# A two-bank rotation for every product of a Gelu stage, its folds by transfers and GpSimd additions, and both halves of the output product in one run

## The chip, the cores and the metric

The kernel runs on one NeuronCore of a Trainium2 chip. The metric is the device time of one execution in microseconds (us). The engines are named as the profile names them: PE (TensorE, matrix products), PEld (its weight loads), ACT (ScalarE), DVE (VectorE), POOL (GpSimd), and SP (SyncE, which issues nearly all transfers here). Each engine works through its own list of instructions in order; the lists meet only at semaphores.

## The reference, cut to what matters

The program is two blocks of a network over `x` of 32 images, 256 channels, 14 by 14 points. The change lies in the last part, a mixture of experts over 8 heads of 32 channels, 16 experts each, on 6272 tokens:

```
h = x @ Wm + bm
t = h.reshape(bs * L_ * H, HD)                      # H = 8 heads of HD = 32
w = softmax(t @ expert_emb); topw, topi = top_k(w, 2)
hmid = gelu(einsum('td,edi->tei', t, W1) + b1)      # 16 experts, 128 hidden each
eo = einsum('tei,eio->teo', hmid, W2) + b2          # back to 32 per head
comb = (sel * topw[:, :, None]).sum(axis=1)         # sel: eo at the two best experts
out = comb.reshape(bs, L_, d) @ Wo + bo             # then added to the residual
```

The kernel computes all 16 experts and multiplies each by a gate that is zero except at the two best, so the sum over `sel` is a sum over the 16 experts.

## The kernel before, in words

The Gelu stage is the last part of the program and takes its last 900 us or so. Its work is cut into 49 **units** of 1024 columns (256 tokens by 4 heads; the last unit has 128 tokens by 8 heads). Each unit has 4 **groups** of 4 experts, so there are 196 groups. The order of the work is a loop over **slots** k on every engine: slot k holds the first products of group k and the second products of group k-1.

- `first(m)` (L2265, PE): for expert m the product with W1, 2 matmuls of 512 columns, into one of three double banks of PSUM, `psA`. ACT's Gelu (L2326) reads that double bank and writes `hid`. `first` waits until the Gelu three experts back is done.
- `second(g, b)` (L2275, PE): for half b (512 columns) of group g the products of its four experts with W2, side by side in the array, into one of two single banks, `psY`. `weigh` (L2347, DVE) adds b2, multiplies by the gates and frees the bank. A plain slot on PE is first, first, first, second half 0, first, second half 1.
- The first group of a unit is weighed into `gacc`, the other three into two buffers `gsum`, and POOL adds each of these to `gacc` (L2254). `weigh` of a unit's last group waits for POOL's addition of the group two before it (`Q["acc"]` at `a - 1`): it writes into that buffer.
- `fold` (L2286, PE): four matmuls with a matrix of ones and zeros add up the four groups of 32 partitions of `gacc` (four experts apart) and put the heads in their places, into a `psY` bank; `combine` (L2356, DVE) copies the 256 columns to `comb`. It runs in slot 4w+6.
- `last` (L2296, PE) and `finish` (L2363, DVE): the product with Wo for 256 tokens, half m_ of the output channels in each of two slots (8c+11 and 8c+12), then bias and residual; SP stores it (L2241). `fold` and `last` take their turn in the `psY` banks as well.
- The routing of later tokens runs alongside: 16 small DVE steps per chunk (`route`, L1625 to L1648), four transposes (L1661), a copy, and a store of the gates.
- SP's list per slot: at every fourth slot `heads_load` (L2205, 4 transfers), then `gates_load` for group k+2 (L2215, 4 transfers, into one of three buffers; it waits until group k-1 is weighed), then the stores of that slot. Waits are put into the list by a helper at L48.

Of the kernel before, what the change touches and what calls it, by code (L numbers as in the profile page):

```python
# [81 lines left out]
def build(nc, x, c1T, c2T, c3T, invts, lut1, lut2, lut3, bn1, bn2, bn3, routerT, w_moe,  # L82
          se_w1T, se_b1, se_w2T, se_b2, se_wgT, se_bg, wm, bm, emb, w1, b1, w2, b2, wo, bo, out):
    with ExitStack() as ctx:
# [990 lines left out]
        Q = {k: sem(f"q_{k}") for k in ("w", "w2", "wo", "set", "hi", "mm1", "gel", "put", "got", "acc", "rt")}  # L1075
# [4 lines left out]
        q_st = [sem(f"q_st{a}") for a in range(2)]  # L1080
        w1_r = sb("w1_r", [128, NE, HID], F32R)
# [3 lines left out]
        foldm = sb("fold", [128, HD])  # L1085
# [523 lines left out]
        def gates_ps(use):  # L1609

            return ps4[:, 3, 64:64 + CH] if use < EARLY else psY[use % 2]
# [44 lines left out]
        def route_pe(eng, r, use):  # L1656

            wait(eng, Q["rt"], (r + 1) * RT2)
            wait(eng, Q["got"], use if r < EARLY else use - 1)
# [63 lines left out]
        with nc.Block() as block:  # L1723
# [34 lines left out]
            def _(eng):  # L1758
# [4 lines left out]
                eng.memset(foldm[:], 0.0).then_inc(Q["set"], 1)  # L1763
                for r in range(4):
                    eng.wait_ge(Q["set"], r + 3)

                    eng.affine_select(out=foldm[:], in_=foldm[:], compare_op=ALU.not_equal, fill=1.0,
                                      base=-32 * r, pattern=[[-1, HD]], channel_multiplier=1).then_inc(Q["set"], 1)
# [368 lines left out]
        comb = ex[:].rearrange("p h c -> p (h c)")[:, 0:2 * UT].rearrange("p (a c) -> p a c", a=2)  # L2137
# [4 lines left out]
        psA = [ctx.enter_context(nc.psum_tensor(f"psA{a}", [128, NB * BLK], F32)) for a in range(3)]  # L2142
        psY = [ctx.enter_context(nc.psum_tensor(f"psY{a}", [128, BLK], F32)) for a in range(2)]
# [5 lines left out]
        FOLD = {4 * w + 6: w for w in range(NU)}  # L2149
        LAST = {8 * c + 11 + m_: (c, m_) for c in range(len(PARTS) - 1) for m_ in range(2)}  # L2150
        LAST.update({4 * NU + 3 + m_: (len(PARTS) - 1, m_) for m_ in range(2)})
# [4 lines left out]
        for r in reversed(range(EARLY, T)):  # L2156
            over = min(over, NEEDED[r] - 6)
            while over + 2 in FOLD or over + 2 in LAST:
                over -= 1
# [3 lines left out]
            clear = [k for k in range(over, over + PACE) if k + 1 not in LAST]  # L2163
# [5 lines left out]
        EXTRAS, EXTRA_USE, BLOCK_USE, uses = {}, {}, {}, EARLY  # L2169
        for k in range(SLOTS):  # L2170
            EXTRAS[k] = [kind for kind, table in (("last", LAST), ("route", ROUTE), ("fold", FOLD)) if k in table]
            for kind in EXTRAS[k]:
                EXTRA_USE[kind, k] = uses
                uses += 1
            for b in range(NB if 0 < k <= NG else 0):
                BLOCK_USE[k - 1, b] = uses
                uses += 1

        def apart(k):

            return not EXTRAS[k] or (EXTRAS[k] == ["fold"] and k + 1 not in LAST)

# [13 lines left out]
        def tokens(c):  # L2196
            tok, n = PARTS[c]
            return V[:].rearrange("p h t c -> p h (t c)")[:, :, tok:tok + n]

# [18 lines left out]
        with nc.Block() as block:  # L2218
            @block.sync
            def _(eng):  # L2220
# [5 lines left out]
                for k in range(SLOTS):  # L2226
# [6 lines left out]
                    if k + 2 < NG:  # L2233

                        wait(eng, q_wst, stored_gates(sum(need <= k + 2 for need in NEEDED)))
                        gates_load(eng, k + 2)
                    if k in LAST:
                        c, m_ = LAST[k]
                        wait(eng, Q["got"], EXTRA_USE["last", k] + 1)
                        for image, at_, off, n in STORES[c]:  # L2240
                            eng.dma_start(out[image, m_ * 128:(m_ + 1) * 128, at_:at_ + n],  # L2241
                                          fin[:, m_, off:off + n]).then_inc(q_st[m_], 16)
# [4 lines left out]
            def _(eng):  # L2247
                for w in range(NU):
                    for g in range(1, 4):
                        a = 3 * w + g - 1  # L2250

# [176 lines left out]
```

## Time and profile before

| what | value |
|---|---|
| median of 3 runs | 2328.03 us (2325.78 to 2329.89) |
| the profiled execution, its own time | 2325.96 us |
| its span in the profile | 2324.2 us |
| busy share of the span: PE, DVE, ACT, POOL | 88%, 58%, 55%, 36% |
| Gelu instructions (ACT L2326) | 784, 809.7 us busy |

The profiled execution is 2.07 us below the median of the three runs, and its span leaves 1.76 us of its time uncovered. Busy shares are averages over stages with different limits. In the last 900 us ACT and PE are the busy ones. SP's issuing instructions are not counted as busy; how full SP is has to be read from its timeline and its waits.

### The profile page before, as it was taken

The page shows a single profiled execution, that of the slowest core. Times are in us where ns is not written, and L with a number is a line of the kernel's source. Part 1 is how long each engine was busy: PE and PEld are TensorE (multiplying, and loading weights), DVE is VectorE, ACT ScalarE, POOL GpSimd, SP SyncE. Part 2 cuts the span into 40 slices and gives each one's busy share as a digit, 9 for nine tenths or more (in the row PEclk, how much of TensorE's full clock was granted, in tenths as well). Part 3 has the DMA queues.
Part 4 walks back from the last instruction along what each step waited for, and adds up shares of the span by engine and source line. Part 5 has one row for each costly group of instructions (what it writes and reads, how often), then busy time and mean ns, then how long its engine had stood idle before and what let it go on. Part 6 is the DMA issues. An engine that isn't in the chain of part 4 may idle for free. (4 is left out here: it accounts for less than half of the span.)

```text
span 2324.2 us, 36023 instructions
## 1 busy us (share of the span) xinstructions
PE 2050.6 (88%) x12850; PEld 1136.7 (49%) x12851; DVE 1336.8 (58%) x2117; ACT 1286.3 (55%) x1634; POOL 831.9 (36%) x608
## 2 busy tenths in 40 slices
PE   6999699999796783798499986999999999999998
PEld 3444355555454562677266553444444444444444
DVE  5666435554456874222388963666666666667533
ACT  3444312222354331122245425999989989999897
POOL 4333111211000777000688611444334443343443
PEclk8999869999798765999689988999999999999999
DMA  2110121220613442677324325666565666556654
GB/s 57 29 29 15 48 85 58 67 69 20 245 55 113 142 146 77 170 210 207 102 83 136 118 73 154 157 158 165 157 164 157 156 162 165 162 152 158 158 155 106
DMA packets 280563, 281.24 MB, mean 121 GB/s; under 512 B 44998, under 2 KB 261654, under 8 KB 280278
## 3 DMA queue, kind: packets, MB, share of 16 engines
q1 hardware_dynamic: 246422, 233.49, 36.6%
q0 software_dynamic: 12288, 25.72, 3.7%
q10 hardware_dynamic: 21696, 19.93, 2.5%
q8 instruction: 99, 1.62, 0.3%
q14 instruction: 58, 0.48, 0.1%
HBM read 203.76 MB, written 75.25 MB: 120 GB/s over the span
## 5 line engine op out<-in xcount | busy, mean ns | idle before, releaser
L2326 ACT ACTIVATE BIG<-psA,b_s 128x1024 f32<-128x1024 f32 x784 | 809.7, 1116 | 88.7 <-PE psA L2265 81.1
L2254 POOL TENSOR_TENSOR BIG<-BIG 128x1024 f32<-128x1024 f32 x147 | 359.4, 2445 | 552.1 <-DVE BIG L2347 552.1
L2265 PE MATMUL psA<-x_r,w_r 128*128 128x512 f32 x1568 | 479.7, 427 | 20.3 <-DMA x_r<-hs_d 12.1
L2347 DVE SCALAR_TENSOR_TENSOR BIG<-psY,b_s,BIG 128x512 f32<-128x512 f32 x392 | 291.6, 750 | 246.2 <-PE psY L2275 245.4
L2265 PEld LDWEIGHTS psA<-x_r,w_r 128*128 128x128 f32 x1568 | 268.7, 190 | 329.4 <-ACT BIG L2326 248.2
L2275 PE MATMUL psY<-BIG,w_s 128*32 128x512 f32 x3136 | 399.9, 600 | 3.6 <-DVE BIG L2347 2.9
L719 DVE TENSOR_REDUCE b_nm<-psN 112x32 f32<-112x512 f32 x128 | 83.1, 686 | 148.0 <-PE psN L616 147.6
L1199 POOL DMA_INDIRECT xg_d<-xnb,SLOT x128 | 135.1, 1056 | 80.8 <-DVE SLOT L1314 44.2
L1774 POOL DMA_INDIRECT gath<-yg_d,SLOT x128 | 140.1, 1095 | 38.5 <-issue 35.7
L2275 PEld LDWEIGHTS psY<-BIG,w_s 128*32 128x32 f32 x3136 | 73.5, 108 | 161.2 <-issue 90.5
L719 DVE TENSOR_REDUCE a_nm<-psN 98x32 f32<-98x512 f32 x128 | 82.4, 686 | 87.5 <-PE psN L607 87.3
L557 POOL CAST b_pat_r<-BIG 72x3584 fp32r<-72x3584 f32 x16 | 50.7, 3171 | 219.5 <-PE psN L616 212.6
L1535 PE MATMUL ps<-BIG,xv 128*128 x528 | 126.6, 383 | 2.2 <-ACT xv L1561 1.0
L1561 ACT ACTIVATE xv<-ps 128x512 f32<-128x512 f32 x66 | 39.4, 597 | 157.5 <-PE ps L1521 155.7
L775 ACT ACTIVATE b_exs<-ps 128x1568 f32<-128x1568 f32 x32 | 47.3, 1477 | 104.6 <-PE ps L585 104.6
L580 PE MATMUL ps<-BIG,b_wb 72*128 72x392 f32 x256 | 101.0, 541 | 4.0 <-DVE xv L725 4.0
L1535 PEld LDWEIGHTS ps<-BIG,xv 128*128 128x128 f32 x528 | 96.1, 192 | 14.2 <-issue 3.7
L1576 DVE COPY ex<-ps 128x512 f32<-128x512 f32 x33 | 22.8, 692 | 99.7 <-PE ps L1535 99.7
L616 PE MATMUL psN<-b_wb_r,b_pat_r 73*112 73x128 f32 x512 | 70.6, 285 | 9.3 <-POOL b_pat_r L557 8.5
L1521 PE MATMUL ps<-ident,xv 128*128 128x128 f32 x264 | 41.3, 281 | 41.1 <-DMA xv<-xg_d 25.3
L616 PEld LDWEIGHTS psN<-b_wb_r,b_pat_r 73*112 73x112 f32 x512 | 61.0, 193 | 30.3 <-DVE b_nm L719 13.4
L795 ACT ACTIVATE BIG<-psMO 128x196 f32<-128x196 f32 x32 | 10.7, 334 | 109.3 <-PE psMO L640 109.3
(394 smaller groups left out, 3192.8 us busy)
## 6 DMA issues: line engine op xcount, KB each, us to landing
BIG<-wt_d SPq DMA_DIRECT2D x784, 128.0 KB, 3.3
x_r<-hs_d SPq DMA_DIRECT2D x196, 128.0 KB, 3.6
xg_d<-ex SPq DMA_DIRECT2D x64, 264.0 KB, 3.7
xv<-xg_d SPq DMA_DIRECT2D x66, 256.0 KB, 3.2
BIG<-ypad_d SPq DMA_DIRECT2D x140, 120.0 KB
xv<-x SPq DMA_DIRECT2D x64, 196.0 KB, 2.7
hs_d<-xv SPq DMA_DIRECT2D x32, 392.0 KB, 3.3
yg_d<-ex ACTq DMA_DIRECT2D x33, 256.0 KB, 3.6
```

The source lines that it names most:

```text
L557: eng.tensor_copy(pat_r[0:KP].rearrange("p g (b r) -> p g b r", b=IMGS), pat[s % 3][:, :, :, 0:HH * PADW]).then_inc(S["vr"], 1)
L580: eng.matmul(ps4[:, i, 0:CH], w_, src, start=True, stop=False)
L616: mm = eng.matmul(psN[0:SR, bank, g * 128:(g + 1) * 128], pat_r[0:KR, bank * 4 + g, sub * SR:(sub + 1) * SR], wb_r[0:KR, bank * 4 + g], st ...
L719: eng.tensor_reduce(dst, src, AX.X, ALU.max, negate=True).then_inc(S["max"], 1)
L1199: eng.indirect_dma_start(xg_d.ap(), bass.IndirectOffsetOnAxis(ap=SLOT[:, t * NSUB + s, j:j + 1], axis=0), xnb[:, t % XB, s], None).then_in ...
L1535: m = eng.matmul(psZ[:, u, r * C:(r + 1) * C], xt[:, u, r, h * 128:(h + 1) * 128], w_moe_s[:, bass.ds(e * (2 * C) + h * C, C)], start=(h = ...
L1774: eng.indirect_dma_start(gath[:, c % GB, 2 * s + j], None, yg_d.ap(), bass.IndirectOffsetOnAxis(ap=SLOT[:, c * NSUB + s, j:j + 1], axis=0) ...
L2254: eng.tensor_tensor(gacc[:, w % 2], gacc[:, w % 2], gsum[:, a % 2], ALU.add).then_inc(Q["acc"], 1)
L2265: mm = eng.matmul(psA[m % 3][:, b * BLK:(b + 1) * BLK], w1_r[:, m % 16], x_r[:, w % 2, b * BLK:(b + 1) * BLK], start=True, stop=True)
L2275: mm = eng.matmul(psY[use % 2][32 * e:32 * e + 32, :], w2_s[:, g % 4 * 4 + e], hid[:, (4 * g + e) % 8, b * BLK:(b + 1) * BLK], start=True, ...
L2326: eng.activation(hid[:, m % 8], psA[m % 3][:], ACT.Gelu, bias=b1_s[:, m % 16:m % 16 + 1]).then_inc(Q["gel"], 1)
L2347: eng.scalar_tensor_tensor(out=dst, in0=psY[use % 2][:], scalar=b2_s[:, g % 4:g % 4 + 1], in1=wb[:, g % 3, b * BLK:(b + 1) * BLK], op0=ALU ...
```

## The change

In the Gelu stage every product takes its turn in one rotation of four double banks `psA` (8 banks, all of PSUM). Five are taken per slot: four by `first` and one by both halves of `second`. On PE a slot becomes four `first` and then both halves of `second` in one run. The fourth `first` of a slot gets the double bank that the second products of the slot before used, so it waits for both their `weigh`. The output product and the transposes of the routing go into the double bank of the second products of the slot before as a guest.

The fold by matmul goes away, with its matrix and `combine`. In its place SP moves `gacc` with 16 transfers per unit (32 for the last), each 32 partitions by 256 columns from SBUF to SBUF (`fold_move`, in slot 4w+5 behind `gates_load`), and POOL adds the four parts with two additions (`fold_add`), ahead of its first addition of the next unit. Both halves of the output product are one run of four matmuls in one slot of eight (8c+13), and `finish` handles both. On DVE the routing steps of a slot stand ahead of its `weigh`.

The diff, cut to its core (unchanged parts of functions and the tables' helpers left out):

```diff
-        psA = [ctx.enter_context(nc.psum_tensor(f"psA{a}", [128, NB * BLK], F32)) for a in range(3)]
-        psY = [ctx.enter_context(nc.psum_tensor(f"psY{a}", [128, BLK], F32)) for a in range(2)]
+        PAIRS_PS = 4
+        psA = [ctx.enter_context(nc.psum_tensor(f"psA{a}", [128, NB * BLK], F32)) for a in range(PAIRS_PS)]
...
-        FOLD = {4 * w + 6: w for w in range(NU)}
-        LAST = {8 * c + 11 + m_: (c, m_) for c in range(len(PARTS) - 1) for m_ in range(2)}
+        FOLDED = {4 * w + 5: w for w in range(NU)}
+        LAST = {8 * c + 13: c for c in range(len(PARTS) - 1)}
...
+            for e in range(4):
+                if k < NG:
+                    FIRST_PAIR[4 * k + e] = take("gel", 4 * k + e + 1)
+                for kind in EXTRAS[k] if e == 0 else ():
+                    EXTRA_USE[kind, k] = uses
+                    guest = k - 2 < NG
+                    PAIR_OF[uses] = PAIR_OF[BLOCK_USE[k - 2, 0]] if guest else take("got", uses + 1)
...
+            if 0 < k <= NG:
+                pair = take("got", uses + NB)
...
+        def wait_pair(eng, pair):
+
+            if pair >= PAIRS_PS:
+                reader, count = TAKEN[pair - PAIRS_PS]
+                wait(eng, Q[reader], count)
...
+        def fold_move(eng, w):
+
+            tok, n, head, heads = UNITS[w]
+            wait(eng, Q["acc"], 3 * w + 3)
+            wait(eng, Q["comb"], w - 1)
+            for e in range(4):
+                for q in range(heads):
+                    eng.dma_start(fold4[q % 4 * 32:q % 4 * 32 + 32, w % 2, e, q // 4 * n:(q // 4 + 1) * n],
+                                  gacc[32 * e:32 * e + 32, w % 2, q * n:(q + 1) * n]).then_inc(q_fold[w % 2], 16)
...
+                    if k in FOLDED:
+                        fold_move(eng, FOLDED[k])
...
+                def fold_add(w):
+                    tok, n, head, heads = UNITS[w]
+                    f = fold4[:, w % 2]
+                    wait(eng, q_fold[w % 2], folded(w))
+                    eng.tensor_tensor(f[:, 0:2], f[:, 0:2], f[:, 2:4], ALU.add).then_inc(Q["half"], 1)
+                    wait(eng, Q["half"], w + 1)
...
+                    eng.tensor_tensor(dst, parts[0], parts[1], ALU.add).then_inc(Q["comb"], 1)
+
                 for w in range(NU):
                     for g in range(1, 4):
                         a = 3 * w + g - 1
+                        if g == 1 and w > 0:
+                            fold_add(w - 1)
 
                         wait(eng, Q["got"], done_group(4 * w + g))
                         wait(eng, Q["acc"], a)
                         eng.tensor_tensor(gacc[:, w % 2], gacc[:, w % 2], gsum[:, a % 2], ALU.add).then_inc(Q["acc"], 1)
+                fold_add(NU - 1)
...
-                def last(c, m_, use):
+                def last(c, use):
                     n = PARTS[c][1]
 
-                    wait(eng, Q["got"], max(use - 1, EXTRA_USE["fold", 4 * min(2 * c + 1, NU - 1) + 6] + 1))
-                    for h in range(2):
-                        mm = eng.matmul(psY[use % 2][:, 0:n], wo_s[:, h, m_ * 128:(m_ + 1) * 128], comb[:, h, 0:n],
-                                        start=(h == 0), stop=(h == 1))
+                    wait(eng, Q["comb"], min(2 * c + 2, NU))
+                    wait_room(eng, use)
+                    for m_ in range(2):
+                        for h in range(2):
...
-                        if e == 2 and "fold" in EXTRAS[k]:
-                            fold(FOLD[k], EXTRA_USE["fold", k])
-                        for b in range(NB if 0 < k <= NG else 0):
-                            if e == (2 + b if apart(k) else 2):
-                                second(k - 1, b)
+                    for b in range(NB if 0 < k <= NG else 0):
+                        second(k - 1, b)
```

How the lists of instructions move, at three places. On **SP**, in slots 12 to 14; `BIG<-wt_d` are the gates, `xv<-BIG` the fold transfers, `out<-BIG` the stores, `wt_d<-wts` the stores of the routing. Before, from the stores of slot 12 to the gates of slot 14:

```order
L2241 DMA out<-BIG 128x196 [waits a_vr]
L2241 DMA out<-BIG 128x60
L1674 DMA wt_d<-wts 128x240 [waits a_vr]
L1674 DMA wt_d<-wts 128x152
L2215 DMA BIG<-wt_d 32x4x256 [waits a_vr,a_tr]
L2215 DMA BIG<-wt_d 32x4x256 x3
L2215 DMA BIG<-wt_d 32x4x256 [waits a_vr,a_tr]
L2215 DMA BIG<-wt_d 32x4x256 x3
```

With the change, from the gates of slot 13 to those of slot 14:

```order
L2261 DMA BIG<-wt_d 32x4x256 [waits a_vr,a_sc]
L2261 DMA BIG<-wt_d 32x4x256 x3
L2243 DMA xv<-BIG 32x256 [waits a_tr,a_nsc]
L2243 DMA xv<-BIG 32x256 x15
L2290 DMA out<-BIG 128x196 [waits a_vr]
L2290 DMA out<-BIG 128x60
L2290 DMA out<-BIG 128x196
L2290 DMA out<-BIG 128x60
L2261 DMA BIG<-wt_d 32x4x256 [waits a_vr,a_sc]
L2261 DMA BIG<-wt_d 32x4x256 x3
```

Sixteen transfers, behind one wait, now stand between one group's gates and the next; the stores of both halves stand together behind them.

On **POOL** the whole stage before was one row of additions into `gacc`:

```order
L2254 TENSOR_TENSOR BIG<-BIG 128x1024 [waits a_vr]
L2254 TENSOR_TENSOR BIG<-BIG 128x1024 [waits a_nsc,a_vr] x146
```

With the change (the rows of `xv` are `fold_add`, the wait of the first is the one for the transfers):

```order
L2310 TENSOR_TENSOR xv<-xv 128x256 [waits a_nrm,a_max]
L2320 TENSOR_TENSOR BIG<-BIG 128x1024 [waits a_nsc,a_vr] x3
L2301 TENSOR_TENSOR xv<-xv 128x512 [waits a_ld0]
L2310 TENSOR_TENSOR xv<-xv 128x256 [waits a_nrm,a_max]
L2320 TENSOR_TENSOR BIG<-BIG 128x1024 [waits a_nsc,a_vr] x3
```

Each unit's three additions now stand behind the two of the fold of the unit before.

On **PE**, in and around the slot with the output product (`x_r` rows are `first`, `BIG` rows `second`, `wo_s` rows the output product):

```order
L2343 MATMUL psA<-BIG,w_s 32x512 x8
L2332 MATMUL psA<-x_r,w_r 128x512 x2
L2355 MATMUL psA<-xv,wo_s 128x256 x4
L2332 MATMUL psA<-x_r,w_r 128x512 x6
L2343 MATMUL psA<-BIG,w_s 32x512 x8
L2332 MATMUL psA<-x_r,w_r 128x512 x8
L2343 MATMUL psA<-BIG,w_s 32x512 x8
```

The second products are one run of eight per slot, and the output product stands once, four matmuls behind the first `first` of its slot.

## Rows read from the trace of the kernel before

**Rows 1.** The page's first line.

```profile
span 2324.2 us, 36023 instructions
```

**Rows 2.** The page's costliest groups (busy us, mean ns, idle before and releaser).

```profile
L2326 ACT ACTIVATE BIG<-psA,b_s 128x1024 f32<-128x1024 f32 x784 | 809.7, 1116 | 88.7 <-PE psA L2265 81.1
L2254 POOL TENSOR_TENSOR BIG<-BIG 128x1024 f32<-128x1024 f32 x147 | 359.4, 2445 | 552.1 <-DVE BIG L2347 552.1
```

**Rows 3.** Busy time by engine in one stretch, granted clock, DMA share, GB/s.

```profile
1740.00:1840.00 100.00, 99.12 (x600) 44.22 (x592) 65.00 (x86) 90.51 (x89) 41.11 (x17) 1.00 0.59 157
```

**Rows 4.** Timeline of PE in a plain slot (start us, us).

```profile
1817.36 1.06 PE L2275 MATMUL psY<-BIG,w_s 128*32 128x512 f32 x8
...
1818.36 0.73 PE L2265 MATMUL psA<-x_r,w_r 128*128 128x512 f32 x2
...
1819.02 1.07 PE L2275 MATMUL psY<-BIG,w_s 128*32 128x512 f32 x8
...
1821.61 1.07 PE L2275 MATMUL psY<-BIG,w_s 128*32 128x512 f32 x8
```

**Rows 5.** Who waited for whom on SP: us in total, times, longest.

```profile
SPq L48 <- DVE BIG L2347: 337.2, 159, 7.4
```

**Rows 6.** Timeline of SP, 11 issues without a wait and the next.

```profile
1803.57 1.38 SPq L2241 DMA_DIRECT2D out<-BIG  x3
1804.99 1.90 SPq L2205 DMA_DIRECT2D x_r<-hs_d  x4
1806.99 1.81 SPq L2215 DMA_DIRECT2D BIG<-wt_d  x4
1808.85 1.38 SPq L2241 DMA_DIRECT2D out<-BIG  x3
```

**Rows 7.** Line L1732, small transfers of 32 partitions (ns min/median/max).

```profile
L1732 SPq DMA_DIRECT2D embd<-emb x4: 421/423/517, 1114.1 to 1115.5; - x4
```

**Rows 8.** Line L2241, the stores of the output, and their landing.

```profile
L2241 SPq DMA_DIRECT2D out<-BIG x112: 332/431/1713, 1475.1 to 2322.2; - x112
...
DMA to landing us min/median/max: 1.6/2.9/4.7
```

**Rows 9.** Groups of POOL by shape, a shorter addition.

```profile
L540 POOL TENSOR_TENSOR a_xh<-xv 128x392 f32<-128x392 f32 x16 | 16.5, 1031 | 0.0
```

**Rows 10.** Timeline around a slot with an output product before.

```profile
1833.45 1.02 PE L2296 MATMUL psY<-ex,wo_s 128*128 128x256 f32 x4
...
1834.51 0.48 DVE L2363 SCALAR_TENSOR_TENSOR BIG<-psY,bo_s,V 128x256 f32<-128x256 f32 x1 [1.22 <-PE psY L2296]
...
1835.34 1.92 PE L2275 MATMUL psY<-BIG,w_s 128*32 128x512 f32 x16
...
1836.57 1.51 DVE L2347 SCALAR_TENSOR_TENSOR BIG<-psY,b_s,BIG 128x512 f32<-128x512 f32 x2 [1.57 <-PE psY L2275]
...
1838.16 2.38 POOL L2254 TENSOR_TENSOR BIG<-BIG 128x1024 f32<-128x1024 f32 x1 [2.41 <-DVE BIG L2347]
```

**Rows 11.** Timeline: group 4 weighed, the last group weighed, the last output product.

```profile
1446.35 0.75 DVE L2347 SCALAR_TENSOR_TENSOR BIG<-psY,b_s,BIG 128x512 f32<-128x512 f32 x1 [0.84 <-PE psY L2275]
...
2314.14 1.51 DVE L2347 SCALAR_TENSOR_TENSOR BIG<-psY,b_s,BIG 128x512 f32<-128x512 f32 x2 [1.05 <-PE psY L2275]
...
2319.74 2.07 PE L2296 MATMUL psY<-ex,wo_s 128*128 128x128 f32 x8 [0.55 <-DVE ex L2356]
```

**Rows 12.** Stretches with granted clock (columns as in rows 3), around two idle times of PE.

```profile
821.90:828.60 6.70, 4.13 (x25) 2.67 (x23) 6.32 (x16) 4.19 (x9) 5.10 (x5) 1.00 0.66 210
828.70:845.60 16.90, 15.11 (x71) 11.79 (x72) 12.46 (x33) 4.65 (x9) 12.50 (x11) 0.50 0.36 107
...
1417.40:1422.50 5.10, 5.08 (x12) 3.44 (x12) 0.00 (x0) 3.82 (x4) 0.00 (x0) 0.50 0.89 221
```

**Rows 13.** Timeline of PE, the work after these two idle times.

```profile
830.49 1.02 PE L1454 MATMUL psN<-ones_c,MS 98*32 98x1 f32 x16 [4.46 <-DVE MS L1269]
...
1417.42 6.18 PE L2265 MATMUL psA<-x_r,w_r 128*128 128x512 f32 x14 [12.07 <-DMA x_r<-hs_d]
```

## What the change will do to the time

> **What bounds the kernel now.** I read the views from the outside in. The page says that the span of 2324.2 us is the whole measure but for 1.76 us [rows 1]; the change touches the Gelu stage alone. There a stretch of 100 us in mid-stage shows PE busy for 99.1, ACT for 90.5, DVE 65.0 and POOL 41.1, at a granted clock of 1.00, which is 2.4 GHz [rows 3]. ACT's 784 Gelu take 809.7 us, 1.033 each, so four of them need 4.13 us [rows 2]. The timeline of PE has a plain slot at 1821.61 - 1817.36 = 4.25 us, and in it each change between first and second products costs something: 1.06 us stands for 8 second products, and 1.00 passes before the first products start [rows 4]. Group 4 is weighed at 1446.35 + 0.75 = 1447.10, the last group, 195, at 2314.14 + 1.51 = 2315.65 [rows 11]: 191 groups in 868.55 us, 4.55 each, **18.19 us for a unit of four**. ACT would need 16.5. The extras (fold, output product, routing) and the small PE losses make up the difference, so PE with its order is the bound, and up to 1.7 us per unit could be had.
>
> The engine that looks idle everywhere in the page is SP. It isn't: it waited for `weigh` for 337.2 us in all [rows 5]; the stage lasts some 900, so more than half of SP's time is spent issuing. Eleven issues without a wait, stores, heads and gates, went from 1803.57 to the start of the next at 1808.85: 5.28 / 11 = **0.48 us per issue** [rows 6]. Before, the stage has 20 per unit and 112 stores [rows 8], 49 x 20 + 112 = 1092; the change adds 48 x 16 + 32 = 800. All 1892 at 0.48 make 908 us, already the length of the whole stage, before SP waits for anything.
>
> **The change, part by part.**
>
> *The two-bank rotation and the single run of second products* remove two of four changes per slot and allow ACT three Gelu ahead. By itself this leads towards ACT's 4.13 us per slot. One run of four for the output product in place of two runs of two saves some changes more. The matmul folds leave PE and `combine` leaves DVE. All that is worth at most 1.7 us per unit, about 80 us, if nothing else ends later. It does.
>
> *The folds by transfers* add 16 issues per unit to SP. The first waits for POOL's last addition of the unit, but it stands behind the gates of slot 4w+5, and these wait until group 4w+4 is weighed. From that moment, all at times per unit:
> - SP resumes, about 0.1 (POOL resumes 0.08 after the end of `weigh`, 1838.16 against 1836.57 + 1.51 [rows 10]); 4 gate issues and 15 fold issues start before the last one: 19 x 0.48 = 9.1. Issues of 32 partitions took 421 to 517 ns at L1732 [rows 7], so a small transfer is no cheaper to issue.
> - The last transfer lands. No transfer from SBUF to SBUF is in the trace. The nearest are the stores out of SBUF, 1.6 us at best, 2.9 in the median [rows 8]. Without DRAM at either end I take 2.3, the middle; 1.6 and 2.9 are the bounds.
> - POOL adds 512 and then 256 columns: between 1.031 for 392 [rows 9] and 2.39 for 1024 (its usual duration, 2.38 in [rows 10]; the mean is 2.445 [rows 2]) a column costs 2.15 ns, so 1.29 and 0.74.
> - Only then may POOL add group 4w+5 into `gacc`, 2.39. That addition stands behind the fold in its list.
> - `weigh` of group 4w+7 waits for it, since both use one `gsum` buffer: 1.5 for two halves [rows 10]. Three hand-overs at 0.08: 0.2.
>
> Sum: 0.1 + 9.1 + 2.3 + 1.29 + 0.74 + 2.39 + 1.5 + 0.2 = **17.6 us from weigh 4w+4 to weigh 4w+7**, three groups, which at ACT's pace would take 12.4. Behind this wait DVE stands; PE has issued three `first` of the next slot and waits with the fourth for the double bank that `weigh` hasn't read; ACT runs dry.
>
> Then the fourth `first` and the run of second products follow: 0.66 from a first to the second products behind it (1819.02 - 1818.36 [rows 4]), and 1836.57 + 1.51 - 1835.34 = 2.74 from the start of that run to the end of its `weigh` [rows 10]. 3.4 in all, so a cycle is **21.0 us** instead of 18.19. In every second cycle the output product stands in that slot, as a guest in the same bank. It can start when the first half is read (0.75 before the end of `weigh`), takes about 1.87 (twice the 1.02 for two matmuls [rows 10], less one start), then `finish` twice 0.48 and its hand-overs: the fourth `first` is 2.3 later, a cycle of **23.3**.
>
> From weigh 4 to weigh 192 there are 47 cycles, 24 plain and 23 with an output product: 504 + 536 = 1040. Then 17.6 to weigh 195. The tail before took 2324.2 - 2315.65 = 8.6. With the change: POOL's last two additions, back to back from 1.5 before that end, are done 2 x 2.39 - 1.5 = 3.3 after it; 31 of 32 fold issues 14.9; the last lands 2.3 later; two additions 2.0; then as before from the last product to the end, 2324.2 - 2319.74 = 4.5 [rows 11]. 27 us. So 1447.1 + 1040 + 17.6 + 27 + 1.8 uncovered = **2533** at an undisturbed clock.
>
> *The clock.* PE would idle once per cycle, for 17.6 - 12.4 = 5 us, less what it still does: 4 to 5. In the trace of before PE idled 4.46 us until 830.49 [rows 13]; the granted clock was 1.00 to 828.6 and 0.50, 1.2 GHz, from 828.7 on, for 17 us [rows 12]. At the start of the Gelu stage PE began at 1417.42 and had 0.50 until 1422.5, 5.1 us [rows 12, 13]; 14 matmuls of `first` took 6.18 there, 0.44 each; at full clock, half of it. The work right after the wait is the work on the path: two matmuls of `first`, 0.44 longer, and 16 second instructions, which take 1.92 [rows 10] against 1.06 for 8 [rows 4], so 0.86 per eight, 1.72 that doubles. 2.16 us per cycle, say 2.15. I take it for 40 of the 48 waits: 86 us. **2533 + 86 = 2619, say 2620.**
>
> Here a page of the Trainium skill would price the landing otherwise. "DMA: Bandwidth & Descriptors", in its section on the anatomy of one DMA, fits a fixed 2.0 us plus bytes over 436 GB/s, on GpSimd's path; that makes an estimate of 2.08 us for 32 KB. With it the sum would be 0.22 x 48 = 11 us less, 2609; no row here shows such a transfer, and the stores' median is longer.
>
> What costs nothing: `combine` and the smaller order changes on DVE (it waits some 5 us per cycle); the gate loads that the folds push back (8 us later, but three buffers, nine or more us ahead, and a longer cycle cover them; if the cover goes, `weigh` waits for gates instead, at the same place); five small POOL instructions of the setup.
>
> **The rivals.**
>
> *Full clock throughout.* If idle times of 4 to 5 us spread so that the clock holds, the sum is 2533; with the landing at 1.6 it is 2533 - 48 x 0.7 = 2500. Against it: the two places in [rows 12].
>
> *The transfers are cheap to issue, and the kernel gets faster.* The place is SP between the gates of slots 4w+5 and 4w+6. If an issue from SBUF to SBUF cost much less than 0.48, the wait would vanish: plain and output cycles average 22.1 and must fall to 18.19 less the longer tail's 0.4, so by 4.3, and 16 issues at 0.21 are the point from which it decides. At 0.1 the floor is ACT's 16.5 plus half of 2.3: 17.7 per unit, 47 x 0.5 = 23 us gained, 6 given back at the tail, 2309. For it: only that no such transfer is in the trace. Against it: no issue near 0.21, and the 32-partition transfers of [rows 7] at 0.42.
>
> *The wait is shorter, SP is the bound.* With issues at 0.35 the cycle loses 19 x 0.13 = 2.5 us, 2533 - 119 = 2414, and the idle times get too short for the clock. For it: the shortest store issues in [rows 8], 332 ns. Against it: the median there, 431.
>
> **How the numbers follow.** The forecast, wait plus lower clock, 0.66. Full clock 0.22. Shorter wait at 2400 to 2480, 0.08. Cheap issues, faster, 0.03; a balance that lands within 0.2% of before (about what a measurement of this kernel can tell from no change) 0.01. The range takes the first two: below 2500, opened to 2490; above all 48 waits at the lower clock and some of the output products with it (8 x 2.15 + 24 x 1.0 = 41), and the landing at 2.9 (48 x 0.6 = 29): 2690, opened to 2700. Faster 0.03, same 0.01, slower 0.96. Against the profiled execution's 2325.96 this is +294 us, and against the median of 2328.03 +292.
>
> **What would show it.** POOL's 128x512 addition should wait for transfers, and DVE's `weigh` for POOL, some 5 us once per unit; SP's wait for `weigh` should fall to a few us per unit; fold issues at 0.48; units of 21 and 23 us in turn, 2 more where the granted clock is below 1; ACT's busy time unchanged at about 810. A stage with ACT near 16.5 us per unit and SP with room would prove it wrong, and issues at 0.2 would say why. A clock of 1.00 throughout would make it 2530.

## The result and the profile after

The changed kernel takes **2723.6 us** (median of 4 runs, 2718.72 to 2728.85); the kernel before took 2326.91 in the runs beside it (4 runs, 2318.90 to 2329.89). The ratio is 1.1712, with a 95% interval of 1.1671 to 1.1752. Slower was forecast, for the mechanism that the trace shows, but the time lies 24 us above the range's upper end of 2700.

From the page of the changed kernel, its first line and four of the costliest groups, as in [rows 1, 2]:

```profile
span 2716.8 us, 35911 instructions
...
L2382 ACT ACTIVATE BIG<-psA,b_s 128x1024 f32<-128x1024 f32 x784 | 799.6, 1140 | 467.2 <-PE psA L2332 466.4
L2403 DVE SCALAR_TENSOR_TENSOR BIG<-psA,b_s,BIG 128x512 f32<-128x512 f32 x392 | 289.8, 750 | 705.6 <-POOL BIG L2320 402.2
...
L2320 POOL TENSOR_TENSOR BIG<-BIG 128x1024 f32<-128x1024 f32 x147 | 349.7, 2379 | 41.8 <-DVE BIG L2403 27.4
L2301 POOL TENSOR_TENSOR xv<-xv 128x512 f32<-128x512 f32 x49 | 61.8, 1262 | 822.4 <-DMA xv<-BIG 822.4
```

ACT's work is what it was, 799.6 us for 784 Gelu against 809.7, but ACT now sat idle for 467.2 us before them instead of 88.7. POOL's additions used to wait for DVE for 552.1 us. They wait for 41.8 us in all now; the first fold addition, in the same list, waits for the transfers instead, 822.4 us, and `weigh` (L2403) waits for POOL.

The same 100 us of mid-stage as in [rows 3] (busy PE, PEld, DVE, ACT, POOL, granted clock, DMA share, GB/s):

```profile
1740.00:1840.00 100.00, 75.89 (x404) 36.05 (x404) 39.40 (x60) 65.20 (x64) 31.78 (x17) 0.87 0.53 129
```

Every engine is less busy than before and the clock is 0.87 on average. No engine that the page counts as busy is the bound. The waits (total us, times, longest), the last line from SP's own list, to be held against [rows 5]:

```profile
POOL xv L2301 <- DMA xv<-BIG: 822.4, 49, 21.7
ACT BIG L2382 <- PE psA L2332: 466.4, 95, 10.8
DVE BIG L2403 <- POOL BIG L2320: 402.2, 49, 10.8
...
PE psA L2355 <- DVE BIG L2403: 168.5, 24, 8.6
...
SPq L48 <- DVE BIG L2403: 220.8, 69, 6.6
```

402.2 us in 49 waits is one wait of `weigh` per unit. That this is close to the kernel's loss of 396.7 us is in part chance, since the loss has three parts. From the end of `weigh` of group 4 to the last instruction the profile is 405 us longer. With "weigh 4w+4" for the end of `weigh` of that group, the first of the unit behind unit w, the stretch from weigh 4w+4 to weigh 4w+7 has 48 x 5.91 of it (19.49 against 13.58), the rest of the cycle 47 x 2.07 (6.68 against 4.61), and the end of the program 24. The chain behind the first part is read from the timeline of one unit and of the output product behind the next wait, SP's, POOL's, DVE's and PE's lines in turn (start us, us, engine, line, what, how many, idle before and releaser); the last four lines are the end of the program.

```profile
1748.97 1.73 SPq L2261 DMA_DIRECT2D BIG<-wt_d  x4
...
1750.80 10.01 SPq L2243 DMA_DIRECT2D xv<-BIG  x16
...
1762.14 1.26 POOL L2301 TENSOR_TENSOR xv<-xv 128x512 f32<-128x512 f32 x1 [17.50 <-DMA xv<-BIG]
...
1763.48 0.72 POOL L2310 TENSOR_TENSOR xv<-xv 128x256 f32<-128x256 f32 x1
1764.16 7.34 POOL L2320 TENSOR_TENSOR BIG<-BIG 128x1024 f32<-128x1024 f32 x3
1766.59 1.41 DVE L2403 SCALAR_TENSOR_TENSOR BIG<-psA,b_s,BIG 128x512 f32<-128x512 f32 x2 [8.71 <-POOL BIG L2320]
...
1768.05 1.22 PE L2332 MATMUL psA<-x_r,w_r 128*128 128x512 f32 x2 [6.26 <-DVE BIG L2403]
...
1769.20 3.55 PE L2343 MATMUL psA<-BIG,w_s 128*32 128x512 f32 x16
...
1793.54 3.38 PE L2355 MATMUL psA<-xv,wo_s 128*128 128x256 f32 x8 [8.12 <-DVE BIG L2403]
...
2682.87 1.41 DVE L2403 SCALAR_TENSOR_TENSOR BIG<-psA,b_s,BIG 128x512 f32<-128x512 f32 x2 [9.79 <-POOL BIG L2320]
...
2687.78 20.36 SPq L2243 DMA_DIRECT2D xv<-BIG  x32
...
2709.42 1.26 POOL L2301 TENSOR_TENSOR xv<-xv 128x512 f32<-128x512 f32 x1 [21.67 <-DMA xv<-BIG]
...
2711.53 2.08 PE L2355 MATMUL psA<-xv,wo_s 128*128 128x128 f32 x8 [24.06 <-POOL xv L2310]
```

Group 4w+4 is weighed at 1748.90. SP then issues four gates and 16 fold transfers, one after the other, until 1760.8; at 1762.14 the last has landed and POOL starts; its first addition of the unit is done at 1766.6 and `weigh` of group 4w+7 can run. PE resumes at 1768.05, after 6.26 us of waiting, and its second products take 3.55 us against 1.92 for the same sixteen in [rows 10].

The granted clock around this wait (columns as above):

```profile
1748.90:1761.80 12.90, 12.89 (x76) 5.65 (x74) 5.83 (x9) 12.90 (x13) 0.00 (x0) 1.00 0.29 81
...
1765.60:1772.40 6.80, 4.35 (x18) 1.10 (x18) 2.75 (x4) 1.11 (x1) 5.61 (x3) 0.51 1.09 232
1772.50:1790.00 17.50, 12.93 (x78) 5.74 (x74) 6.93 (x10) 13.17 (x13) 1.73 (x2) 0.99 0.40 101
```

PE ran at 2.4 GHz until it had to wait, at 1.2 GHz from the middle of the wait until some 4.4 us after it resumed, then at 2.4 again. This happened in each of the 48 cycles, for 6.8 to 10.2 us.

### The profile page after: what moved, and what is told of

It is laid out like the page before. It is cut to its first block and busy times, and to the rows that moved or that the text cites. A ratio compares the mean times of both kernels' runs of the same rounds, so it can differ in the third digit from the quotient of the medians.

```text
span 2716.8 us, 35911 instructions
## 1 busy us (share of the span) xinstructions
PE 2100.7 (77%) x12450; PEld 1185.8 (44%) x12451; DVE 1245.0 (46%) x2068; ACT 1276.7 (47%) x1634; POOL 915.1 (34%) x701
## 5 line engine op out<-in xcount | busy, mean ns | idle before, releaser
L2382 ACT ACTIVATE BIG<-psA,b_s 128x1024 f32<-128x1024 f32 x784 | 799.6, 1140 | 467.2 <-PE psA L2332 466.4
L2403 DVE SCALAR_TENSOR_TENSOR BIG<-psA,b_s,BIG 128x512 f32<-128x512 f32 x392 | 289.8, 750 | 705.6 <-POOL BIG L2320 402.2
L2332 PEld LDWEIGHTS psA<-x_r,w_r 128*128 128x128 f32 x1568 | 289.4, 203 | 388.7 <-ACT BIG L2382 128.9
L2343 PE MATMUL psA<-BIG,w_s 128*32 128x512 f32 x3136 | 405.4, 637 | 1.6 <-ACT BIG L2382 1.3
L2320 POOL TENSOR_TENSOR BIG<-BIG 128x1024 f32<-128x1024 f32 x147 | 349.7, 2379 | 41.8 <-DVE BIG L2403 27.4
L2301 POOL TENSOR_TENSOR xv<-xv 128x512 f32<-128x512 f32 x49 | 61.8, 1262 | 822.4 <-DMA xv<-BIG 822.4
L2355 PE MATMUL psA<-xv,wo_s 128*128 128x256 f32 (+1 forms) x200 | 90.5, 632 | 192.6 <-DVE BIG L2403 168.5
L2343 PEld LDWEIGHTS psA<-BIG,w_s 128*32 128x32 f32 x3136 | 89.1, 114 | 210.3 <-issue 138.5
L2355 PEld LDWEIGHTS psA<-xv,wo_s 128*128 128x128 f32 x200 | 62.1, 329 | 216.5 <-issue 178.7
L1535 PEld LDWEIGHTS ps<-BIG,xv 128*128 128x128 f32 x528 | 96.1, 192 | 13.7 <-issue 3.1
L616 PEld LDWEIGHTS psN<-b_wb_r,b_pat_r 73*112 73x112 f32 x512 | 61.0, 193 | 31.6 <-DVE b_nm L719 13.4
```

The lines of the kernel that those rows point to most:

```text
L616: mm = eng.matmul(psN[0:SR, bank, g * 128:(g + 1) * 128], pat_r[0:KR, bank * 4 + g, sub * SR:(sub + 1) * SR], wb_r[0:KR, bank * 4 + g], st ...
L1535: m = eng.matmul(psZ[:, u, r * C:(r + 1) * C], xt[:, u, r, h * 128:(h + 1) * 128], w_moe_s[:, bass.ds(e * (2 * C) + h * C, C)], start=(h = ...
L2301: eng.tensor_tensor(f[:, 0:2], f[:, 0:2], f[:, 2:4], ALU.add).then_inc(Q["half"], 1)
L2320: eng.tensor_tensor(gacc[:, w % 2], gacc[:, w % 2], gsum[:, a % 2], ALU.add).then_inc(Q["acc"], 1)
L2332: mm = eng.matmul(psA[FIRST_PAIR[m] % PAIRS_PS][:, b * BLK:(b + 1) * BLK], w1_r[:, m % 16], x_r[:, w % 2, b * BLK:(b + 1) * BLK], start=Tr ...
L2343: mm = eng.matmul(bank_pair(use)[32 * e:32 * e + 32, b * BLK:(b + 1) * BLK], w2_s[:, g % 4 * 4 + e], hid[:, (4 * g + e) % 8, b * BLK:(b + ...
```

## The experiments

**The theory.** SP's serial issue of 16 fold transfers, between `weigh` of group 4w+4 and POOL's addition, ends last in every unit; its price per issue was set too low. **Rivals:** the transfers' landing, not their issue; the lower clock alone; the rotation and the single run themselves; and, for the price, that it is SP's usual one plus other work in between.

The runs with half of the transfers, the five forms, the filler and POOL's later additions are one execution each; the other times are medians of four or five. In the profiles of all these kernels the first load of the stage is issued between 1405.1 and 1417.5 us, although the program up to there is the same. So the stage is also compared from the end of `weigh` of group 4 to the last instruction: 877.1 us before, 1282.1 with the change.

### Half of the transfers

```diff
...
-            for e in range(4):
+            for e in range(2):
                 for q in range(heads):
                     eng.dma_start(fold4[...
...
-                    eng.tensor_tensor(f[:, 0:2], f[:, 0:2], f[:, 2:4], ALU.add)...
+                    eng.tensor_tensor(f[:, 0:2], f[:, 0:2], f[:, 0:2], ALU.add)...
```

> Only 8 of the 16 fold transfers per unit are issued (two of the four experts' parts; the first of POOL's two additions adds a part to itself), all else as in the changed kernel. My theory: the loop from the gates of slot 4w+5 over SP's 16 issues of 0.633 us, the landing, POOL's three additions and the weigh of group 4w+7 sets the cycle. Eight issues less shorten it by 8 x 0.633 = 5.1 us in 48 cycles: 2719 - 243 = 2476 if the clock still falls in each cycle, 2373 if the idle time gets too short for that; between 2360 and 2490. Rival one: the landing and POOL set it, or the weigh that the fourth first product waits for, and the number of issues does not: 2700 to 2720. Rival two: SP as a whole is full and sets it: 800 - 400 issues less, the same 243, but then no wait of weigh for POOL would be left and SP would not wait for weigh at all.

Measured: 2415.06 us, within the range. From the first to the last fold issue it took 4.42 us instead of 9.79 (mean of 48 units), from weigh 4w+4 to 4w+7 14.57 instead of 19.49, and the cycles, plain and with an output product, 18.4 and 21.4. `weigh` waited less for POOL:

```profile
DVE BIG L2403 <- POOL BIG L2320: 190.6, 48, 5.6
```

Eight transfers fewer per unit are worth 308.5 us, 6.3 per unit; 5.4 of it is their issue time. The landing of the last didn't get shorter (2.17 against 1.86), and the shorter wait gives back some of the clock (0.96 in the stretch from 1500 to 2200, 0.86 with the change). The number of issues sets the time.

### Where the transfer begins and ends

Units 5 to 47 take turns at five forms, each with 16 transfers of 32 KB.

```diff
+            kind = w % 5 if 5 <= w < NU - 1 else 0
...
+                    if kind == 1:
+                        eng.dma_start(dst, hs_d.ap()[0, 32 * q:32 * q + 32, tok:tok + n])...
+                    if kind == 2:
+                        eng.dma_start(scrap.ap()[e, 32 * q:32 * q + 32], gacc[32 * e:32 * e + 32, w % 2, q * n:(q + 1) * n])...
+                    if kind == 3:
+                        eng.dma_start(dst, gacc[32 * q:32 * q + 32, w % 2, e * n:(e + 1) * n])...
+                    if kind == 4:
+                        eng.dma_start(fold4[:, w % 2, e, 64 * q:64 * q + 64], gacc[:, w % 2, e * n + 64 * q:e * n + 64 * q + 64])...
```

> The fold transfers of units 5 to 47 take one of five forms by w mod 5, all 32 KB and 16 per unit, so outputs are not the reference's: 0 as in the change; 1 from DRAM (32 partitions); 2 from SBUF to DRAM; 3 from SBUF to SBUF with the same partitions at both ends; 4 from SBUF to SBUF with 128 partitions of 256 bytes. Open: why a fold issue takes 0.633 us where other issues take 0.474. Theory one, SBUF at both ends: forms 0, 3 and 4 at 0.63, forms 1 and 2 at 0.47. Theory two, 32 partitions of 1 KB: forms 0 to 3 at 0.63, form 4 at 0.47. Theory three, the step from one group of partitions to another: form 0 alone at 0.63. The units with cheap forms should have cycles shorter by 15 x 0.16 = 2.4 us, and a time of about 2719 - 17 x 2.4 = 2680 under theory one.

Measured: 2671.22 us. The issues by line (ns min/median/max; L2247 as in the change, L2249 from DRAM, L2251 to DRAM, L2253 between the same partitions, L2255 with 128 partitions of 256 bytes):

```profile
L2247 SPq DMA_DIRECT2D xv<-BIG x256: 507/591/1803, 1439.1 to 2660.2; - x128
...
L2249 SPq DMA_DIRECT2D xv<-hs_d x144: 307/421/484, 1594.8 to 2607.0; - x144
...
DMA to landing us min/median/max: 1.7/1.9/3.6
...
L2251 SPq DMA_DIRECT2D scrap<-BIG x144: 373/421/1077, 1616.5 to 2629.5; - x144
...
DMA to landing us min/median/max: 1.6/1.6/3.4
...
L2253 SPq DMA_DIRECT2D xv<-BIG x128: 507/591/1632, 1640.9 to 2529.9; - x128
...
L2255 SPq DMA_DIRECT2D xv<-BIG x128: 516/601/1485, 1666.3 to 2557.1; - x128
```

421 ns with DRAM at one end, 591 to 601 with SBUF at both; from one start to the next 0.464 and 0.633 (0.644 for L2255). Among these forms neither the shape nor a shift between partitions matters much. Units with SBUF at both ends took 19.4 to 19.8 us from weigh 4w+4 to 4w+7 (median), those from DRAM 16.6, those to DRAM 16.4: 15 x 0.169 = 2.5 of the 2.9 between the form of the change (19.5) and the one from DRAM is the issue. This is the price that the prediction took from the wrong kind of transfer.

### PE kept busy in the wait

The first products that stand before the wait are repeated, 30 matmuls instead of two, so that PE doesn't idle.

```diff
+                    k = m // 4
+                    held = k % 4 == 1 and k >= 9 and m % 4 == (0 if EXTRAS[k] else 2)
-                    for b in range(NB):
+                    for b in list(range(NB)) * (15 if held else 1):
```

> In the slot in which PE waits (4w+9) the product that PE issues last before the wait is repeated 15 times into the same bank, some 6 us of array time, so PE works through most of the wait; results are unchanged. My theory: the granted clock falls because PE idles there and costs 2.15 us per cycle behind the wait: with the filler the clock stays at 1.00, the stretch from weigh 4w+4 to weigh 4w+7 stays at 19.5, the rest of the cycle falls from 5.6 and 7.7 to about 3.5 and 5.6, 2719 - 100 = 2620 (2600 to 2650). Rival: the lower clock is no cost, since the path is on SP, POOL and DVE: 2719 or, as ACT starts the third Gelu of that slot later, up to 2750.

Measured: 2659.81 us, above the expected range; of the 100 us that the theory gave, 59 came. The clock stayed at 1.00 from 1500 to 2200, and the rest of a cycle, from weigh 4w+7 to 4w+8, fell by 1.84 us, from 5.62 and 7.78 to 3.75 and 5.99. But the wait itself grew by 0.57, to 20.06: to the first fold issue 2.02 against 1.92, 15 issues 10.02 against 9.79, the landing 2.00 against 1.86, POOL and `weigh` 5.95 against 5.86. The usual pace of the issues stayed at 0.633, but 33 units, not 23, had a pause of over 0.9 us in them. The clock costs about 1.84 x 47 = 86 us here, and only on top of the wait, which it doesn't cause. Why the wait is longer in this one execution stays open.

### POOL's fold additions later

They move from ahead of the unit's first addition to ahead of its third. In the second version the output product also moves on, from slot 8c+13 to 8c+14.

```diff
-                        if g == 1 and w > 0:
+                        if g == 3 and w > 0:
                             fold_add(w - 1)
...
-        LAST = {8 * c + 13: c for c in range(len(PARTS) - 1)}
+        LAST = {8 * c + 14: c for c in range(len(PARTS) - 1)}
```

> All 16 transfers stay; POOL does the two fold additions behind the second addition of the next unit instead of ahead of its first, so the weigh of group 4w+7 no longer waits for the transfers. My theory: the wait of weigh for POOL goes, and SP's list becomes the bound: 20 issues at 0.474, 16 at 0.633 and some 3.2 stores make 21.1 us per unit against 26.2 now, so 2719 - 48 x 5 = 2480; between 2440 and 2510, with SP's wait for weigh near nothing. Rival: the order on POOL was the only limit, the units run at ACT's 4.05 us per slot plus an output product, 17.4: 2300. Rival: the order on POOL has nothing to do with it: 2719.

Measured: 2604.49 us, 94 us above the range. The wait that was aimed at is gone, weigh 4w+4 to 4w+7 takes 13.7, but the cycles are 21.5 and 25.8. The waits show what took its place:

```profile
DVE BIG L2403 <- DMA BIG<-wt_d: 171.5, 25, 10.7
...
PE psA L2355 <- POOL xv L2310: 95.0, 19, 22.4
```

PE's output product waits for POOL's second fold addition, and `weigh` for gates that stand behind 16 transfers in SP's list.

> The 16 SBUF-to-SBUF transfers with POOL's fold additions behind the second addition of the next unit, and the output product one slot later (8c+14). The run without that second step gave 2604 in place of my 2480: PE waited for the fold additions in the slots of the output product. My theory: with that wait gone SP's list is what is left, 20 issues at 0.474, 16 at 0.633 and 3.2 more, 21.1 us per unit, 21.5 to 22.5 with its waits: 2510, between 2450 and 2545, and weigh waits for gates. Rival: SP has room, the cycles fall to 16.1 and 17.9 as in the run through DRAM: 2290 to 2320.

Measured: 2543.73 us, just inside the range. PE's wait for the fold is nearly gone (27.9 us in 2 waits, 22.2 of it in the last), the gates are what is left, and SP has almost no free time:

```profile
DVE BIG L2403 <- DMA BIG<-wt_d: 305.6, 81, 8.6
...
SPq L48 <- DVE BIG L2403: 17.5, 11, 3.2
```

SP's issues alone, 800 at 0.65 (mean with its pauses) and 1092 at 0.475 (the gates' median), make 1039 us of the 1097.9 from weigh 4 to the end. So even with these waits for the fold out of the way, the kernel with 16 transfers per unit on SP takes 217 us more than the kernel before (2326.74 in the runs beside it).

### The rotation with the fold by matmul

The transfers and POOL's fold additions go; `fold` and `combine` come back in slot 4w+6, as a guest in the double bank, like the output product. In the second version the output product is cut in halves, in slots 8c+12 and 8c+13.

```diff
-        FOLDED = {4 * w + 5: w for w in range(NU)}
+        FOLD = {4 * w + 6: w for w in range(NU)}
...
+                        if e == 0 and "fold" in EXTRAS[k]:
+                            fold(FOLD[k], EXTRA_USE["fold", k])
...
-        LAST = {8 * c + 13: c for c in range(len(PARTS) - 1)}
+        LAST = {8 * c + 12 + m_: (c, m_) for c in range(len(PARTS) - 1) for m_ in range(2)}
```

> The rotation of four double banks, the single run of second products and of the output product stay; the folds are matmuls with a copy on DVE again, as a guest in the same bank, in slot 4w+6, so no fold transfers and no fold additions. My theory: the transfers are the whole loss and the rotation by itself is a gain. In the trace of the changed kernel the slots between two waits follow each other in 4.05 us; four of them, about 0.5 for the fold and 0.6 for the half of an output product give 17.3 us per unit against 18.19 before: 2327 - 48 x 0.9 - 4 for the first slots = 2280, between 2255 and 2310, and the clock stays at 1.00. Rival: the rotation itself costs, since the fourth first product waits for both weigh of the slot before: 2330 or above, with PE waiting for weigh in plain slots.

Measured: 2310.49 us, ratio 0.9936 (0.9913 to 0.9958), 0.5 us above the expected range. From weigh 4 to the end it took 861.1 us, 16.0 less than before; cycles of 17.06 and 18.78, clock 1.00 from 1500 to 2200. So the rotation costs nothing; the whole loss belongs to the folds by transfers and POOL's additions for them. It is worth less than ACT's pace promised, since PE is still full (694.6 of 700 us busy).

> As the rotation with matmul folds, with the output product in two halves in two slots again (8c+12 and 8c+13). It tells what the one run of four is worth within the rotation. In that run a unit with an output product takes 1.7 us more than one without. Two runs of two each cost 1.02 us on PE, two more changes of product and a second hand-over to finish: my theory is 0.3 to 0.8 us more per eight slots, 2310 + 24 x 0.5 = 2322, between 2312 and 2332. Rival: two short guests fit into the slack of two slots, where one long one does not: 2285 to 2308.

Measured: 2295.8 us, ratio 0.9875 (0.9849 to 0.9901): the rival won. From weigh 4 to the end 853.1 us, 8.1 less than with the single run; the remaining 6.6 between the two medians is of the size of the scatter at the stage's start. The single run of four is not what gains here.

### The folds through DRAM, five transfers per unit

`gacc` is stored to DRAM by one transfer in slot 4w+5 and loaded by four in slot 4w+6; POOL's fold additions stand ahead of the third addition.

```diff
-            for e in range(4):
-                for q in range(heads):
-                    eng.dma_start(fold4[...
+            eng.dma_start(gacc_d.ap()[w % 2], gacc[:, w % 2]).then_inc(q_out[w % 2], 16)
...
+            wait(eng, q_out[w % 2], (w // 2 + 1) * 16)
+            for q in range(heads):
+                eng.dma_start(fold4[q % 4 * 32:q % 4 * 32 + 32, w % 2, :, q // 4 * n:(q // 4 + 1) * n],
+                              gacc_d.ap()[w % 2].rearrange("(e p) c -> p e c", p=32)[:, :, q * n:(q + 1) * n])...
...
+                    if k - 1 in FOLDED:
+                        fold_back(eng, FOLDED[k - 1])
```

> The folds go through DRAM: one store of gacc per unit (slot 4w+5) and four loads of 32 partitions by 4 x 256 (slot 4w+6), 5 issues in place of 16, none with SBUF at both ends; POOL's two additions behind the second addition of the next unit. My theory: it is the number and price of SP's issues that make the wait. SP then issues 28 transfers per unit, 13.3 us, the loads land some 10 us behind weigh 4w+4, and neither weigh nor the output product waits for the folds for long: units of about 17.2 us and some 6 us more at the end, 2285, between 2260 and 2340. Rival: two transfers one behind the other have a longer latency than sixteen side by side, the wait stays: above 2450.

Measured: 2395.11 us, ratio 1.0297 (1.0268 to 1.0326), 55 us above the range. Plain cycles are at ACT's pace, 16.13 us, but those with an output product take 22.9, since PE comes to it before POOL has folded:

```profile
PE psA L2364 <- POOL xv L2319: 91.0, 25, 10.3
```

So the output product was put later, first by one slot (8c+14):

> As the run with the folds through DRAM, and the output product one slot later (8c+14 in place of 8c+13). My theory: there the plain cycles already ran at 16.13 us, ACT's pace, and the cycles with an output product took 22.9 only since PE waited for the fold additions in slot 8c+13. One slot later the additions are done: 16.1 plus 1.7 for the four matmuls and finish. 1447 + 24 x 16.15 + 23 x 17.9 + 34 at the end = 2281, plus 1.8: 2283, between 2265 and 2300, faster than before and than the rotation with matmul folds (2310), clock at 1.00. Rival: the output product costs the same wherever it stands, since its place in the double bank makes the fourth first product wait: no change from 2395.

Measured: 2298.5 us, ratio 0.9877 (0.9859 to 0.9895), within the range. Cycles of 16.21 and 18.60. PE still waited a little:

```profile
1897.94 1.99 PE L2364 MATMUL psA<-xv,wo_s 128*128 128x256 f32 x8 [0.93 <-POOL xv L2319]
```

Then by two (8c+15):

> The version with the folds through DRAM and the output product in slot 8c+14 took 2298.5 us; its output-product cycles last 18.60 us, its plain ones 16.21, and in the slot with the output product PE still waited 0.93 us for POOL's second fold addition (the timeline at 1897.94). Here the output product stands one slot later, in 8c+15. Theory: that wait goes and nothing comes in its place; 23 output-product cycles become 0.9 us shorter, 21 us in all: 2278, range 2268 to 2288. Rival: PE's list is full in a plain slot (2.24 for the first products and 1.92 for the second, of 4.03), so the 1.99 of the output product push the cycle however they are placed and the wait only fell into time that would be lost anyway: 2293 to 2303.

Measured: 2275.53 us, ratio 0.9792 (0.9765 to 0.9818). The theory's 2278 fits and the rival's 2293 to 2303 doesn't. From weigh 4 to the end it took 836.0 us, 16.9 less than with slot 8c+14, where the theory had 21. The rest of the 23.0 us between the medians is of the size of the scatter at the stage's start (the first load is 9.8 us earlier in this profile), so that 2278 was met so closely is in part luck. In the timeline the output product starts without a wait:

```profile
1883.87 1.89 PE L2364 MATMUL psA<-xv,wo_s 128*128 128x256 f32 x8
```

Last, the output product in halves, in slots 8c+15 and 8c+16:

> As the version with the output product in slot 8c+15, but in two halves, in slots 8c+15 and 8c+16. With the fold by matmul the same cut took the stretch from the weighing of group 4 to the end from 861.1 to 853.1 us, 8.1 less. Theory: two guests of 1.0 us fit the stage as well here: 8 us less than the version with one run, 2270, range 2258 to 2282. Rival: without the matmul folds PE has room for one run of 2 us already, and each further guest costs its change between products twice: no gain against the version with one run or up to 8 us more, which is 2278 to 2288 if that one comes out at 2278.

Measured: **2272.18 us, ratio 0.9775 (0.9752 to 0.9797)**, within the theory's range. From weigh 4 to the end 828.2 us, 7.8 less than with one run, as in the pair above; the medians differ by 3.4 us and their intervals overlap, so what the cut gains here is not settled by the times. Mid-stage, for the stretch from 1500 to 2200 (columns as above):

```profile
1500.00:2200.00 700.00, 699.05 (x4180) 333.97 (x4173) 474.02 (x584) 674.47 (x661) 390.70 (x207) 1.00 0.88 232
```

PE and ACT are both full at 2.4 GHz. This version is faster than the kernel before and than the changed one.

## Why the prediction's direction held and its range didn't

The measured terms are means over the units of the changed kernel's trace.

| term | predicted us | measured us |
|---|---|---|
| weigh 4w+4 to the first fold issue | 2.0 | 1.92 |
| 15 further fold issues | 15 x 0.48 = 7.2 | 9.79 |
| landing of the last | 2.3 | 1.86 |
| hand-overs, POOL's three additions, `weigh` | 6.1 | 5.93 |
| **weigh 4w+4 to 4w+7** | **17.6** | **19.49** |
| to weigh 4w+8, plain, with the lower clock | 3.4 + 2.15 | 5.62 |
| the same with an output product | 5.7 + 2.15 | 7.78 |
| last `weigh` to the end | 27 | 32.5 |
| group 4 weighed at | 1447.1 | 1434.7 |

- **The mechanism was right.** `weigh` waits for POOL once per unit, POOL for the transfers, and SP for nothing from the gates to the last fold issue; the order of the terms is that of the timeline. Half of the transfers took most of the loss away, and the rotation alone none of it.
- **The step that failed is "0.48 per fold issue"**. Where SBUF is at both ends the issue of such a transfer costs 0.633, shown inside one kernel beside 0.464 for the same bytes with DRAM at one end. 15 x 0.153 = 2.3 of the 2.59 us; the rest are pauses over 0.9 us in 23 of the 48 units, whose cause stays open. It makes 2.59 x 48 = 124 us, and some 4.7 of the longer tail (31 issues). All the rows used for the price [rows 6, 7, 8] are transfers to or from DRAM. The text says that the trace has no transfer from SBUF to SBUF and bounds the landing for that reason on both sides; the issue of the very same transfers was bounded only from below, by rivals at 0.21 and 0.35. The trace of before had dearer issues outside the Gelu stage, 140 loads of another shape with a median of 655 ns, against 431 in [rows 8]:

```profile
L491 SPq DMA_DIRECT2D BIG<-ypad_d x140: 654/655/1422, 278.4 to 534.2; - x140
```

  An upper bound of 0.65 from there would have put 15 x 0.17 x 48 = 122 us on the upper end of the range, and the measured time inside it.
- **The landing** was 0.44 too long, 21 us in the other direction. The Trainium skill, "DMA: Bandwidth & Descriptors", in its section on the anatomy of one DMA, has a fit for GpSimd's path from which the prediction worked out an estimate of 2.08 us for 32 KB. SP's transfers here took 1.86, nearer to that than to the 2.3 taken between the bounds of the stores; no run here has such a transfer on GpSimd's path.
- **The clock** fell in all 48 waits rather than 40. PE's idle time in them was 6.2 to 8.1 us where 4 to 5 were predicted, and `weigh` waited for POOL for 8.2 on average where some 5 were. The rest of the cycles came out 101 us above the 3.4 and 5.7 predicted at full clock, where 86 were taken. Not all of that is the clock: with the filler, at full clock, the rest was 3.75 and 5.99, so the clock's price comes out at 1.84 per cycle rather than 2.15, and the work behind the wait was put 0.3 too short. The two errors nearly cancel, which is luck. The rival with the full clock throughout is refuted by the windows.
- **The start** was 12.4 us earlier. 8.0 of it lies ahead of the first load of the stage, within the scatter of the runs, and 4.7 between that load and the first `weigh`, in the first slots. The second part shows in the profiles of all kernels with the rotation: 13.4 to 14.4 us lie between the two, against 18.2 in the one of before.

The sum again with what was measured: 2619.5 + 48 x 1.87 + 15 + 5.5 - 12.4 = 2717, and the profiled execution took 2718.72.

The rival with cheap issues, which would have been faster, fell with the price. The one in which SP is the bound was refuted as priced, at 0.35 per issue; its mechanism is real, though, at the higher price: with the wait moved out of the way it holds the kernel at 2543.73.

The Trainium skill, "DMA: Bandwidth & Descriptors", in its rules for kernel authors, asks to coalesce many small transfers into one large one, since under 64 KB one pays mostly overhead. The runs agree: with POOL's additions and the output product in the same places (8c+14), five larger transfers per unit took 2298.5 us and 16 of 32 KB 2543.73. The way from 1.17 to 0.98 needed the later places as well.

## What to carry to other kernels

Price an issue by transfers with the same two ends and shape; where the trace has none, bound the issue on both sides as well as the landing. Count the instructions of the issuing engine's list per cycle: an engine that the page shows idle can be the full one, and 16 transfers behind one wait are a serial chain. When a result comes later, move its consumers too: here the same transfers through DRAM were 3% slower with the output product in slot 8c+13 and 2.1% faster two slots on.

## What the runs showed of the hardware

- From one start to the next, transfers of 32 KB with 32 partitions, issued by SP, took 0.633 us with SBUF at both ends and 0.464 with DRAM at one. With SBUF at both ends, 128 partitions of 256 bytes took 0.644. They landed 1.86 us after the start of their issue between SBUF and SBUF, 1.85 from DRAM and 1.57 to DRAM (medians in the run with five forms). DRAM at one end isn't cheap in every shape: the loads at L491 took 655 ns each.
- With waits of some 6 to 8 us of PE in every cycle the clock fell to 1.2 GHz in every cycle and came back each time. Matmuls that filled the wait kept it at 2.4 GHz there, and the work behind the wait was 1.84 us shorter per cycle.
- In the same run the wait itself was 0.57 us longer per cycle: the median issue kept its pace of 0.633 us, but more units had a pause in them (33 against 23), and POOL's 128x1024 additions took 2.41 us on average against 2.38. The cause isn't shown.
